# Key and value trees of a hard feed-forward layer: from all leaves for every token to rows sorted by leaf through DRAM

## The chip, the cores and the metric

The kernel runs on one NeuronCore of one Trainium2 chip, as one launch. The metric is the device time of the launch in microseconds. The kernel before was timed three times: 1565.92, 1569.52 and 1570.98 us, median 1569.52 us.

## The reference, cut to what matters

Four transformer layers work on x of 16 x 256 tokens of 128 features (4096 tokens, 32 tiles of 128). The change is in the feed-forward part of the third layer, in which the queries, keys and values of an attention come each out of a tree of depth 4 with 16 leaves. A token goes down a tree by the signs of node scores, and its leaf alone, a small two-layer perceptron of width 64, acts on it:

```python
def _fff(x, node_w, node_b, w1, b1, w2, b2):
    cur = zeros(N)
    for _ in range(4):
        score = einsum('nd,nd->n', xf, node_w[cur]) + node_b[cur]
        cur = 2 * cur + 1 + (score >= 0)
    sel = one_hot(cur - 15, 16)
    hidden = relu(einsum('nd,ldh->lnh', xf, w1) + b1) * sel.T
    return einsum('lnh,lho->no', hidden, w2) + sel @ b2
q, k, v = _fff(x, q_*), _fff(x, k_*), _fff(x, v_*)
attn = softmax(q @ k.T / sqrt(128))        # within each of the 16 batches of 256 tokens
out = attn @ v
```

x is layer-normalised before it enters, and the result is added to x.

## The kernel before, in words

The program is a row of stages, each a block in which every engine has its own instruction stream and engines meet at semaphores; the end of a block holds all of them. In order of time: attention of layer 0, its feed-forward part, a top-k attention (`attention_top`), a routed mixture of 16 experts (`route_top1`, then `run_experts`), attention of layer 2 (`mha`), the trees (`attention_trees`, lines 2017 to 2338), attention of layer 3, and a quantised linear layer.

**The trees before are dense.** `attention_trees` works in 8 groups (g) of 4 tiles, 512 tokens. For each group 24 steps (k) follow, 8 for each of the three trees: a step takes two leaves, 128 hidden columns in all. `hidden` (lines 2074 to 2085) computes them for all 512 tokens by three products of a high and a low part of the weights and the tokens, and a fourth with a one-hot of the tokens' leaves that adds the bias and pushes the hidden values of foreign leaves far below zero, so that the rectifier kills them. ScalarE takes the rectifier (line 2181), VectorE the low part of the result (`low`, line 2284), and `out` (lines 2087 to 2101) multiplies both with the second weights, three products, added up in PSUM over the 8 steps of a tree. TensorE is one step ahead: in step k it issues `hidden` of k+1 before `out` of k. Between the steps of group g lie, written out by hand with step numbers, the attention of group g-1 (`scores`, `turn`, `attend`, one tile after the other) and the routing of group g+1: transposes of x (line 2055), node scores (line 2061), the decisions and one-hots on VectorE (`route`, lines 2243 to 2279). The middle six groups are a hardware loop. GpSimd and the DMA queues have nothing to do in this stage.

**Where the trees' weights come from.** In the routing stage `route_top1` SP loads the weights of all three trees (line 1866) over the space of the experts' weights; ScalarE makes the high parts (line 1729), and VectorE makes the low parts and the bias matrix in 28 pieces (`tree_piece`, lines 1775 to 1798), one in each of the 28 steps of a binary search (`search`, line 1800), between the count (line 1801) and the wait for TensorE's total (line 1803). SP loads the experts' weights behind the last piece (lines 1876 to 1880).

**The same means elsewhere.** `route_top1` sends 32 tiles of rows to places in DRAM by GpSimd's indirect DMAs (line 1887); `mha` of layer 2 gathers 32 tiles of rows with them (line 783). Line 978 loads a register of VectorE from SBUF, ahead of a branch (line 979).

Of the kernel before, what the change touches and what calls it, by code (L numbers as in the profile page):

```python
# [19 lines left out]
P = 128  # L20
# [1022 lines left out]
def attention_top(core):  # L1043
# [5 lines left out]
    with Stage(core, "top") as st:  # L1049
# [12 lines left out]
        names = "xh bo xTp xT qp q S sc top nm P pk PTp PT Y X bn own zero tick".split()  # L1062
        s = {n: st.sem(n) for n in names}
        rs_act, rs_dve = token_scales(core, st, MV[:, :, 1], RS[:], "a")
# [79 lines left out]

        @blk.gpsimd
        def _(pool):
            def slot(b):
# [485 lines left out]
def route_top1(core, masks):  # L1633
# [7 lines left out]
    with Stage(core, "route") as st:  # L1641
# [5 lines left out]
        WC = STEPS * P  # L1647
        raw_w = [core.EW[:, WC * n:WC * n + WC] for n in range(2)]
        raw_mix = [core.EW[:, 2 * WC:2 * WC + MIXC], core.EW[:, 0:MIXC]]
        t1, t2, t3 = (st.sb(n, [P, MIXC], BF16) for n in ("t1", "t2", "t3"))  # L1650
# [9 lines left out]
        names = "xh xTp xT L own cnt tot thr dx ex mvp MTp rowsp dgr eqr ca prf zst sl zfill high piece t1 t2 t3 bw mix0 mix1".split()  # L1660
# [6 lines left out]
        MIXR = (P, SELP)  # L1667
        PIECE, HALF = STEPS * P // 6, MIXC // 2
# [49 lines left out]
        def _(act):  # L1718
# [14 lines left out]
            for n, rows in enumerate(MIXR):  # L1733
                q = slice(0, rows)
                need(act, s["piece"], 12 + 8 * n)
                act.wait_ge(s[f"mix{n}"], 16)
                act.activation(t1[q, :], raw_mix[n][q, :], ACT.Copy).then_inc(s["t1"], 1)
                act.wait_ge(s["piece"], 12 + 8 * n + 2)
                act.activation(t2[q, :], raw_mix[n][q, :], ACT.Copy).then_inc(s["t2"], 1)
                act.wait_ge(s["t1"], n + 1)  # L1740
                act.activation(t3[q, :], t1[q, :], ACT.Identity, scale=core.w("tree", "part")[q, 0:1]).then_inc(s["t3"], 1)
# [3 lines left out]
        def _(dve):  # L1745
            link = Chain(dve, s["own"])
            dve.memset(ones[:], 1.0)
            dve.memset(core.mix[SELP:P, 1, :], 0.0)
# [26 lines left out]
            def tree_piece(k):  # L1775
                need(dve, s["piece"], k)
                if k < 12:
                    n, c = divmod(k, 6)
# [5 lines left out]
                n, step = divmod(k - 12, 8)  # L1784
                step, h = divmod(step, 2)
                q, at = slice(0, MIXR[n]), slice(HALF * h, HALF * h + HALF)
                part = lambda i: core.w("tree", "part")[q, i:i + 1]
# [911 lines left out]
```

## Time and profile before

| what | value |
|---|---|
| median of three runs | 1569.52 us |
| span of the profiled execution | 1580.8 us |
| instructions in the span | 22619 |
| TensorE busy | 1200.3 us (76%) |
| VectorE busy | 999.1 us (63%) |
| ScalarE busy | 612.1 us (39%) |
| GpSimd busy | 275.6 us (17%) |
| moved by DMA | 69.47 MB |

The span goes from the first to the last instruction of one profiled execution, and is the only time shown of that execution; it lies 0.7% above the median of the runs without a profile. Shares of busy time are means over stages that are bound by different engines. An engine's busy time counts an instruction from its start to its modelled end, and instructions of TensorE overlap, so a row's duration of a product is more than what it adds to a stream of products.

### The profile page before, as it was taken

What the parts mean: (1) busy time and instruction counts of PE and PEld (TensorE: products, weight loads), DVE (VectorE), ACT (ScalarE), POOL (GpSimd) and SP (SyncE); (2) the same over time, 40 slices, a digit from 0 to 9 for tenths busy, and PEclk for the clock granted to TensorE, in tenths of its full rate; (3) what the DMA queues carried; (4) which work ended last, traced back from release to release, by engine and by line L of the source; (5) the groups of instructions that cost most, each with busy time, mean ns of one, the idle gap of its engine ahead of it and who ended that gap; (6) DMA issues with size and microseconds to landing.
All of it is one profiled execution on the core that took longest, in us unless ns stands there. A gap on an engine that the chain in (4) does not pass through costs nothing. (4 is left out here: it accounts for less than half of the span.)

```text
span 1580.8 us, 22619 instructions
## 1 busy us (share of the span) xinstructions
PE 1200.3 (76%) x6805; PEld 876.5 (55%) x6805; DVE 999.1 (63%) x3354; ACT 612.1 (39%) x1154; POOL 275.6 (17%) x330
## 2 busy tenths in 40 slices
PE   4788799999766653335826886999999999758852
PEld 2656599899744452114614554677777777335631
DVE  7777746666558859823266775565556665446768
ACT  3465344444332230112225652434444344236631
POOL 1344001010001000071384430000000000024401
PEclk9899799999965555567956996999999999768985
DMA  7342100000000040312224410000000000024301
GB/s 233 105 124 66 28 1 1 2 0 1 1 1 0 0 161 15 108 47 90 71 81 108 111 44 1 1 1 1 1 1 0 0 1 1 1 67 126 98 5 53
DMA packets 54762, 69.47 MB, mean 44 GB/s; under 512 B 6784, under 2 KB 35712, under 8 KB 54016
## 3 DMA queue, kind: packets, MB, share of 16 engines
q1 hardware_dynamic: 51328, 61.78, 13.5%
q0 software_dynamic: 3328, 6.43, 1.3%
q8 instruction: 48, 0.79, 0.2%
q14 instruction: 58, 0.48, 0.1%
HBM read 44.99 MB, written 23.59 MB: 43 GB/s over the span
## 5 line engine op out<-in xcount | busy, mean ns | idle before, releaser
L2284 DVE SCALAR_TENSOR_TENSOR tree_hl<-tree_pH,tree_hh 128x512 fp32r<-128x512 f32 x192 | 132.3, 689 | 94.5 <-ACT tree_hh L2181 92.8
L790 POOL TENSOR_TENSOR mha_ks<-KS,w_ctx 104x1024 fp32r<-104x1024 f32 (+1 forms) x48 | 90.8, 1893 | 535.4 <-POOLq L100 488.6
L2181 ACT ACTIVATE tree_hh<-tree_pH 128x512 fp32r<-128x512 f32 x192 | 114.6, 597 | 145.7 <-PE tree_pH L2085 145.7
L850 DVE TENSOR_REDUCE mha_nm<-mha_pS 128x16 f32<-128x1024 f32 x96 | 117.1, 1220 | 28.3 <-PE mha_pS L612 24.1
L1432 ACT ACTIVATE ffn_hid<-ffn_pH,w_ffn 128x512 f32<-128x512 f32 x128 | 85.5, 688 | 55.1 <-PE ffn_pH L1355 54.4
L2098 PE MATMUL tree_pY<-tree_hh,w2h 128*128 128x512 f32 x192 | 100.9, 526 | 4.3 <-DVE tree_hl L2284 4.2
L733 ACT ACTIVATE XH<-mha_pST 128x1024 f32<-128x1024 f32 x96 | 97.8, 1018 | 9.9 <-PE mha_pST L633 9.8
L612 PE MATMUL mha_pS<-mha_ks,mha_qs 96*128 96x256 f32 (+1 forms) x384 | 79.9, 335 | 27.5 <-DVE mha_nm L850 17.2
L1368 PEld LDWEIGHTS ffn_pE<-W2R,ffn_hid 128*128 128x128 f32 x768 | 94.6, 194 | 4.4 <-issue 0.2
L1544 DVE SCALAR_TENSOR_TENSOR ffn_acc<-ffn_pE,ffn_wt,ffn_acc 128x128 f32<-128x128 f32 x192 | 54.0, 343 | 66.9 <-PE ffn_pE L1368 66.9
L1368 PE MATMUL ffn_pE<-W2R,ffn_hid 128*128 128x128 f32 x768 | 95.2, 278 | 0.0
L612 PEld LDWEIGHTS mha_pS<-mha_ks,mha_qs 96*128 96x128 f32 (+1 forms) x384 | 59.0, 213 | 43.6 <-issue 23.6
L2082 PE MATMUL tree_pH<-tree_xTh,w1h 128*128 128x512 f32 x192 | 80.8, 421 | 1.0 <-DVE tree_sel L2278 1.0
L2084 PE MATMUL tree_pH<-tree_xTh,w1l 128*128 128x512 f32 x192 | 76.6, 399 | 0.0
L2083 PE MATMUL tree_pH<-tree_xTl,w1h 128*128 128x512 f32 x192 | 76.1, 397 | 0.0
L2098 PE MATMUL tree_pY<-tree_hl,w2h 128*128 128x512 f32 x192 | 75.9, 395 | 0.0
L2085 PE MATMUL tree_pH<-tree_sel,mix 128*128 128x512 bf16 x192 | 75.3, 392 | 0.0
L2098 PE MATMUL tree_pY<-tree_hh,w2l 128*128 128x512 f32 x192 | 75.1, 391 | 0.0
L633 PE MATMUL mha_pST<-mha_qs,mha_ks 104*128 104x256 f32 (+1 forms) x384 | 65.5, 295 | 1.5 <-ACT XH L733 0.4
L642 PE MATMUL mha_pO<-XH,VB 128*18 128x256 f32 x768 | 61.3, 392 | 0.0
L1353 PE MATMUL ffn_pH<-ffn_xTh,up_h 128*128 128x512 f32 x128 | 57.7, 451 | 1.6 <-ACT ffn_hid L1432 1.2
L633 PEld LDWEIGHTS mha_pST<-mha_qs,mha_ks 104*128 104x128 f32 (+1 forms) x384 | 55.2, 199 | 3.3 <-ACT XH L733 1.9
(478 smaller groups left out, 2777.4 us busy)
## 6 DMA issues: line engine op xcount, KB each, us to landing
mha_qs<-queries SPq DMA_DIRECT2D x72, 256.0 KB, 4.1
queries<-mha_qh SPq DMA_DIRECT2D x24, 256.0 KB, 2.1
queries<-mha_ql SPq DMA_DIRECT2D x24, 256.0 KB, 2.4
EW<-in_L_W_dram SPq DMA_DIRECT2D x32, 128.0 KB, 2.5
EW<-in_tree_full_dram SPq DMA_DIRECT2D x2, 1536.0 KB, 7.9
slots_in<-route_zero SPq DMA_DIRECT2D x4, 640.0 KB, 11.7
X<-in_x_dram SPq DMA_DIRECT2D x8, 256.0 KB, 7.3
exp_xe<-slots_in SPq DMA_DIRECT2D x16, 128.0 KB, 2.1
```

The lines of the kernel that those rows point to most:

```text
L612: ins = pe.matmul(pS[:, NH * g:NH * g + NH, :], qs[u][0:KC, g, c0:c0 + P], ks[b % KB][0:KC, g, :, :], start=True, stop=True)
L633: ins = pe.matmul(pST[:, n, :], ks[b % KB][0:K1, g, h0:h0 + 2, :], qs[u][0:K1, g, c0:c0 + S], start=True, stop=True)
L733: act.activation(PT[b % PB][:, CU * i:CU * i + CU, :], pST[:], ACT.Exp, scale=SC).then_inc(s["P"], 1)
L790: pool.tensor_tensor(ks[b % KB][0:K1, :, :, :], kb, hb, ALU.mult).then_inc(s["k"], 1)
L850: dve.tensor_reduce(nm[:, t, :], pS[:], AX.X, ALU.max, negate=True).then_inc(s["nm"], 1)
L1368: ins = pe.matmul(pE[p % 2][:, j, :], hc, core.W2R[:, P * r:P * r + P], start=(c == 0), stop=(c == 1))
L1432: act.activation(hid[p % 2][:, c, :], pH[c][:], ACT.Gelu, bias=b).then_inc(s["h"], 1)
L2082: pe.matmul(pH[k % 2][:], core.w1h[:, k0], xTh[u][:], start=True, stop=False)
L2084: pe.matmul(pH[k % 2][:], core.w1l[:, k0], xTh[u][:], start=False, stop=False)
L2098: ins = pe.matmul(bank[:], w2[:, k0], h[k % 2][:], start=(c == 0 and i == 0), stop=False)
L2181: act.activation(hh[k % 2][:], pH[k % 2][:], ACT.Relu).then_inc(s["h"], 1)
L2284: dve.scalar_tensor_tensor(hl[k % 2][:], pH[k % 2][:], 0.0, hh[k % 2][:], ALU.max, ALU.subtract).then_inc(s["lo"], 1)
```

## The change

The query tree stays dense, with 64 steps instead of 192. For the key and the value tree the tokens are sorted by leaf. Each leaf gets whole tiles of 128 rows, so that 48 tiles (32 + 16) hold all tokens of a tree whatever their leaves are. At the start of the stage all 32 tiles are normalised, transposed and scored, and for each token its row in the sorted order is worked out (`running`, `rank`, `starts`, `places`) and for each sorted tile its leaf (`leaf_table`). GpSimd scatters the 32 tiles of rows to DRAM (`core.tx`), once for each tree. In 12 groups of 4 tiles for each tree SP loads the leaf's weights for every tile (a register loaded from the table gives the address) and the 4 tiles of rows; TensorE transposes them (`rows_T`), multiplies up and down (`up`, `down`) in plain fp32, and SP stores the results to DRAM (`core.ty`). GpSimd gathers them back, 32 tiles for each tree, and the attention follows by batches of two tiles. The order is written in slots (`TreeSlots`): 34 slots with a dense step each, 14 for the keys with 7 dense steps, 14 for the values with 11, and then 16 batches of attention with the last 12 dense steps. The sorted rows' space is cleared in the top-k stage, by 12 DMAs of 512 KB. In the routing stage the 28 pieces become 12, and the experts' loads wait for the 12th.

```diff
 def attention_top(core):
+        @blk.sync
+        def _(sp):
+            sp.wait_ge(s["none"], 1)
+            for q in range(2 * NS // (8 * P)):
+                sorted_rows = core.tx[q % 2].rearrange("(q n p) d -> p q n d", n=8, p=P)
+                sp.dma_start(sorted_rows[q // 2], none[:].unsqueeze(1).to_broadcast([P, 8, P])).then_inc(core.rows_cleared, 16)
+            sp.wait_ge(core.rows_cleared, 16 * (2 * NS // (8 * P)))
...
 def route_top1(core, masks):
-            dve.memset(core.mix[SELP:P, 1, :], 0.0)
...
-                tree_piece(k)
+                if k < PIECES:
+                    tree_piece(k)
...
-            sp.wait_ge(s["piece"], BITS)
+            sp.wait_ge(s["piece"], PIECES)
...
+NJ = T + NLEAF
+NS = NJ * P
+XG = NJ // GT
+class TreeSlots:
+    ALONE, SPAN = 34, XG + 2
+    K0, V0 = ALONE, ALONE + SPAN
+    S0 = V0 + SPAN
+    LAG = 3
+    END = S0 + B + LAG + 1
+    def __init__(self):
+        dense = list(range(self.ALONE))
+        dense += [self.K0 + n for n in range(self.SPAN) if n % 2 == 0]
+        dense += [self.V0 + n for n in range(self.SPAN) if n % 4 != 3]
+        dense += [self.S0 + n for n in range(NG * NCH - len(dense))]
...
 def attention_trees(core):
...
+            def rows_T(i):
+                pe.wait_ge(s_rows[i % 3], 16 * (i // 3 + 1))
...
+                for j in range(GT):
+                    ins = pe.transpose(pA[:, cols_of(j)], xs[i % 3][:, j, :], ident)
+                ins.then_inc(s["tr"], 1)
...
+            def up(i):
+                pe.wait_ge(s_leaf[i % 3], 16 * GT * (i // 3 + 1))
+                pe.wait_ge(s["xsT"], i + 1)
+                need(pe, s["hid"], i)
+                for j in range(GT):
+                    ins = pe.matmul(pU[0:LW, cols_of(j)], leaf[i % 3][:, j, 0:LW], xsT[i % 2][:, cols_of(j)], start=True, stop=True)
+                ins.then_inc(s["up"], 1)
...
+            def down(i):
...
+                pe.wait_ge(s["hid"], i + 1)
+                need(pe, s["ys"], i)
+                for j in range(GT):
+                    ins = pe.matmul(pD[:, cols_of(j)], hid[i % 2][:, cols_of(j)], leaf[i % 3][0:LW + 1, j, LW + 1:LEAFC], start=True, stop=True)
+                ins.then_inc(s["dn"], 1)
...
+            for n in range(at.END):
+                m, b = at.step.get(n), at.batch(n)
+                if m is not None and m + 1 < NG * NCH:
+                    hidden(m + 1)
...
+                for lag, part in enumerate((rows_T, up, down)):
+                    i = at.sparse(n, lag)
+                    if i is not None:
+                        part(i)
+                k = at.batch(n, -1)
+                if k is not None and k % 2 == 0:
+                    keys_T(k // 2)
+                if b is not None:
+                    scores(b)
+                if at.batch(n, 1) is not None:
+                    turn(at.batch(n, 1))
+                if m is not None:
+                    out(m)
+                if at.batch(n, at.LAG) is not None:
+                    attend(at.batch(n, at.LAG))
...
+        @blk.gpsimd
+        def _(pool):
...
+            pool.wait_ge(core.rows_cleared, 16 * (2 * NS // (8 * P)))
+            for n in range(2):
+                pool.wait_ge(s["place"], n + 1)
+                for t in range(T):
+                    pool.indirect_dma_start(core.tx[n], bass.IndirectOffsetOnAxis(ap=place[:, n, t:t + 1], axis=0), XH[:, t, :], None,
+                                            bounds_check=NS - 1, oob_is_err=False).then_inc(s_sent[n], 16)
+            for n in range(2):
+                for u in range(2):
+                    pool.wait_ge(s_out[u], 16 * (n + 1) * XG // 2)
+                    if n == 0:
+                        pool.wait_ge(s_sent[u], 16 * T)
+                for t in range(T):
+                    pool.indirect_dma_start((XH, V)[n][:, t, :], None, core.ty[n], bass.IndirectOffsetOnAxis(ap=place[:, n, t:t + 1], axis=0),
+                                            bounds_check=NS - 1, oob_is_err=False).then_inc(s_got[n][t // GT], 16)
+        @blk.sync
+        def _(sp):
+            def load(i):
+                n, j0 = i // XG, GT * (i % XG)
+                if j0 == 0:
+                    sp.wait_ge(s["table"], n + 1)
+                need(sp, s["dn"], i - 2)
+                for j in range(GT):
+                    of = sp.value_load(table[0:1, NJ * n + j0 + j:NJ * n + j0 + j + 1], min_val=0, max_val=NLEAF - 1)
+                    sp.dma_start(leaf[i % 3][:, j, :], core.A["leaves"][n, bass.ds(of, 1), :, :].rearrange("o p c -> p (o c)")).then_inc(s_leaf[i % 3], 16)
+                if j0 == 0:
+                    sp.wait_ge(s_sent[n], 16 * T)
+                sp.dma_start(xs[i % 3][:], core.tx[n][P * j0:P * j0 + GT_P, :].rearrange("(t p) d -> p t d", p=P)).then_inc(s_rows[i % 3], 16)
+            def store(i):
+                n, j0 = i // XG, GT * (i % XG)
+                sp.wait_ge(s["ys"], i + 1)
+                sp.dma_start(core.ty[n][P * j0:P * j0 + GT_P, :].rearrange("(t p) d -> p t d", p=P), ys[i % 2][:]).then_inc(s_out[i % 2], 16)
+            for n in range(2):
+                for i in range(XG * n, XG * n + XG + 2):
+                    if i < XG * n + XG:
+                        load(i)
+                    if i >= XG * n + 2:
+                        store(i - 2)
+        @blk.vector
...
+            def results(i):
+                dve.wait_ge(s["dn"], i + 1)
+                need(dve, s_out[i % 2], 16 * (i // 2))
+                dve.tensor_copy(ys[i % 2][:].rearrange("p t d -> p (t d)"), pD).then_inc(s["ys"], 1)
...
+            for n in range(at.END):
+                m = at.step.get(n)
+                if m is not None:
+                    low(m)
...
+                if n == 1:
+                    starts(1)
+                    places(1)
+                if n in (2, 3):
+                    leaf_table(n - 2)
+                i = at.sparse(n, 0)
+                if i is not None:
+                    rows_T(i)
+                i = at.sparse(n, 2)
+                if i is not None:
+                    results(i)
+                if at.batch(n) is not None:
+                    shift(at.batch(n))
+                done = at.batch(n, at.LAG)
+                if done is not None:
+                    final(done)
+                    statistics(done)
```

## Rows read from the trace of the kernel before

The rows are in the order in which the prediction comes to them. A row of a timeline gives the start in us from the span's start, the duration in us, the engine, the line of the kernel, the operation, what it writes and reads, its shape and its count; a bracket tells how long the engine idled before it and what released it.

**Rows 1.** Windows of the tree stage: busy us (instructions) per engine, granted clock, DMA share, GB/s
```profile
957.30:973.20 15.90, 5.29 (x20) 3.94 (x21) 9.09 (x27) 0.69 (x2) 0.00 (x0) 0.50 0.00 1
973.20:1354.60 381.40, 377.08 (x1759) 268.32 (x1760) 218.55 (x521) 158.65 (x314) 0.00 (x0) 0.99 0.00 1
1354.60:1369.80 15.20, 9.77 (x38) 6.52 (x37) 6.49 (x28) 4.99 (x14) 0.00 (x0) 0.67 0.00 1
```

**Rows 2.** Groups by line, tree stage: busy us, mean ns, idle before and its releaser
```profile
L2284 DVE SCALAR_TENSOR_TENSOR tree_hl<-tree_pH,tree_hh 128x512 fp32r<-128x512 f32 x192 | 132.3, 689 | 94.5 <-ACT tree_hh L2181 92.8
```

**Rows 3.** Timeline of PE: first matmul of two dense steps, four steps apart
```profile
1344.66 0.39 PE L2082 MATMUL tree_pH<-tree_xTh,w1h 128*128 128x512 f32 x1
...
1351.28 0.40 PE L2082 MATMUL tree_pH<-tree_xTh,w1h 128*128 128x512 f32 x1
```

**Rows 4.** Timeline of DVE, routing stage: start us, duration us
```profile
561.50 0.54 DVE L1748 MEMSET mix<- 64x576 uint32 x1 [0.16 <-issue]
...
595.65 0.69 DVE L1782 TENSOR_TENSOR w1l<-EW,w1h 128x512 fp32r<-128x512 f32 x1
596.41 0.22 DVE L1804 TENSOR_SCALAR route_ge<-route_pC,w_route 128x1 f32<-128x1 f32 x1
```

**Rows 5.** Window in the top-k stage: busy us per engine, granted clock, DMA share, GB/s
```profile
535.00:556.00 21.00, 11.75 (x37) 7.25 (x36) 17.85 (x129) 4.39 (x13) 1.45 (x2) 0.50 0.00 0
```

**Rows 6.** Timeline, start of the tree stage, DVE and PE; brackets: idle before
```profile
957.13 0.18 DVE L904 BATCH_NORM_AGGREGATE MV<-mha_bn 128x2 f32<-128x6 f32 x1
...
960.44 1.11 DVE L2238 TENSOR_SCALAR tree_xh<-X,MV,RS 128x128 f32<-128x128 f32 x4 [3.13 <-PEq L100]
...
963.43 1.95 PE L2061 MATMUL tree_pX<-w_tree,tree_xT 128*128 128x48 f32 x8 [0.70 <-ACT tree_xT L2186]
```

**Rows 7.** Timeline of PE, routing stage: the transposes of two successive groups
```profile
575.94 1.09 PE L1682 MATMUL route_pX<-w_ctx,XH 128*128 128x128 f32 x4
...
578.39 1.09 PE L1682 MATMUL route_pX<-w_ctx,XH 128*128 128x128 f32 x4
```

**Rows 8.** Timeline of DVE: operations of 512 and 192 columns out of PSUM
```profile
594.25 0.69 DVE L1772 COPY route_MT<-route_pM 128x512 f32<-128x512 f32 x1 [1.26 <-PE route_pM L1696]
...
965.41 0.36 DVE L2256 TENSOR_TENSOR tree_zs<-tree_pX,w_tree 128x192 f32<-128x192 f32 x1 [0.33 <-PE tree_pX L2061]
```

**Rows 9.** Timeline of POOL: first and last of 32 scatters; the last of 32 gathers
```profile
669.43 1.22 POOL L1887 DMA_INDIRECT slots_in<-XH,slots  x1 [126.06 <-DVE slots L1856]
...
709.25 0.97 POOL L1887 DMA_INDIRECT slots_in<-XH,slots  x1 [0.30 <-issue]
...
838.81 1.00 POOL L783 DMA_INDIRECT XH<-slots_out,slots  x1 [0.31 <-issue]
```

**Rows 10.** Timeline of SP's queue: two of the 32 expert loads
```profile
651.39 0.47 SPq L1878 DMA_DIRECT2D EW<-in_L_W_dram  x1
651.90 0.43 SPq L1879 DMA_DIRECT2D EW<-in_L_W_dram  x1
```

**Rows 11.** The page's DMA issues: count, size, median us from issue to landing
```profile
mha_qs<-queries SPq DMA_DIRECT2D x72, 256.0 KB, 4.1
...
exp_xe<-slots_in SPq DMA_DIRECT2D x16, 128.0 KB, 2.1
...
out_dram<-X SPq DMA_DIRECT2D x8, 256.0 KB, 2.3
```

**Rows 12.** Timeline of DVE around the register load of line 978
```profile
807.20 0.38 DVE L939 BATCH_NORM_AGGREGATE MV<-mha_gbn 128x2 f32<-128x6 f32 x4
808.42 0.37 DVE L954 TENSOR_SCALAR mha_ve<-MV 128x4 f32<-128x4 f32 x1 [0.84 <-issue]
```

**Rows 13.** Timeline of PE after the last dense step: attention products
```profile
1358.98 0.71 PE L2133 MATMUL tree_pO<-tree_vv,tree_PT 128*128 128x128 f32 x4
...
1364.43 1.06 PE L2133 MATMUL tree_pO<-tree_vv,tree_PT 128*128 128x128 f32 x4
```

**Rows 14.** Windows: the expert loads; the attention tail
```profile
655.00:660.00 5.00, 1.22 (x2) 0.21 (x2) 4.52 (x16) 0.00 (x0) 0.00 (x0) 0.50 0.89 264
...
1360.50:1368.40 7.90, 6.45 (x22) 4.49 (x21) 3.91 (x18) 2.28 (x7) 0.00 (x0) 0.50 0.00 0
```

More of the change, by code:

```diff
@@ L1776, in tree_piece @@
                 need(dve, s["piece"], k)
-                if k < 12:
-                    n, c = divmod(k, 6)
+                if k < 4:
+                    n, c = divmod(k, 2)
                     high, low = halves[n]
@@ L2041, in attention_trees @@
+        nm, sm, rc = (st.sb(n, [P, T]) for n in ("nm", "sm", "rc"))
+        bn = two("bn", [P, 6])
         pH = [st.ps(f"pH{u}", [P, 512]) for u in range(2)]
-        pY = [st.ps(f"pY{u}", [P, 512]) for u in range(2)]
-        names = "xh xTp xT xs np own oh ohp sel zero H h lo c Y y vTp v S nm mx P PTp PT O rc X bn mv tick".split()
+        pZ = st.ps("pZ", [P, 4, 512])
+        pS, pT = st.ps("pS", [P, 512]), st.ps("pT", [P, 512])
+        pY, pA, pU, pD = (pZ[:, n, :] for n in range(4))
+        names = "const early full ones xh xTp xT np go own hot ran cnt rank place table xs ohp sel H h lo c Y y tr xsT up hid dn ys ktp kt S nm P PTp PT O rc X bn".split()
@@ L2213, in group @@
-            def group(g, u):
-                for k in range(STEPS):
-                    hidden(g, u, k)
-                    if k == 0 and past(g):
-                        out(g - 1, 1 - u, 2)
-                    if k in (NCH, 2 * NCH):
-                        out(g, u, k // NCH - 1)
-                    if past(g):
-                        attention(g - 1, 1 - u, k)
-                    if k == 14 and more(g):
-                        x_evac(g + 1, 1 - u)
-            rs_act(act)
-            x_evac(0, 0)
@@ L2331, in _, with normalise @@
-            normalise(0, 0)
-            dve.memset(oh[:], 0.0).then_inc(s["zero"], 1)
-            rs_dve(dve)
-            for step in range(7):
-                route(0, 0, step)
-            group_slots(dve, group)
-            for k in range(STEPS):
-                attention(NG - 1, 1, k)
-MAGIC = 1.5 * 2.0 ** 23
+            link = Chain(dve, s["own"])
+            def normalise(g):
+                for t in range(GT * g, GT * g + GT):
+                    ins = dve.tensor_scalar(XH[:, t, :], X[:, t, :], MV[:, t, 0:1], RS[:, t:t + 1], ALU.subtract, ALU.mult)
+                ins.then_inc(s["xh"], 1)
@@ new lines, in statistics @@
+            def statistics(b):
+                dve.wait_ge(s["X"], b + 1)
+                for t in range(TB * b, TB * b + TB):
+                    ins = dve.bn_stats(bn[t % 2][:], X[:, t, :])
+                ins.then_inc(s["bn"], 1)
+                dve.wait_ge(s["bn"], b + 1)
+                for t in range(TB * b, TB * b + TB):
+                    dve.bn_aggr(MV[:, t, :], bn[t % 2][:])
+            for u in range(2):
+                ins = dve.memset(hid[u][LW:LW + 1, :], 1.0)
+            ins.then_inc(s["ones"], 1)
@@ new lines, in _ @@
+            ins.then_inc(s["hot"], 1)
+            link(path(2, 2))
+            running(1)
+            starts(0)
+            places(0)
+            for n in range(at.END):
+                m = at.step.get(n)
+                if m is not None:
+                    low(m)
+                    g, c = divmod(m, NCH)
+                    if c == 3 and 1 <= g < NG - 1:
+                        split(g + 1)
+                if n == 1:
[7 more added lines that the diff above has]
+                i = at.sparse(n, 2)
+                if i is not None:
+                    results(i)
+                if at.batch(n) is not None:
+                    shift(at.batch(n))
[3 more added lines that the diff above has]
+                    statistics(done)
```

602 lines of the change are left out of this document (327 added, 275 removed).

## The prediction

> **What bounds the kernel now.** I read first the engines and the time slices of the page: TensorE is 76% busy, but its share moves from stage to stage, so no mean over the span prices this change. The page's chain that ended last covers a few per cent only, inside the last stage, and says nothing of the trees. Then I took windows around the tree stage, the only large one that the diff rebuilds [rows 1]: from 957.3 to 1369.8 us, 412.5 us, of which 381.4 are dense steps with TensorE 377.1 us busy at full clock and no transfer at all. The groups by line show who waits there: ScalarE and VectorE idle for TensorE, and VectorE's `low`, 0.689 us a step, for ScalarE [rows 2]; the reader is to see that TensorE is the bound. The timeline gives the price of a dense step: 6.62 us for four, so 1.655 us [rows 3].
>
> **The change, part by part.**
>
> Gone: 128 of 192 dense steps, 128 x 1.655 = 212 us of a full engine. This is the whole gain; the rest is what is put in its place.
>
> *Routing stage.* The 16 pieces that go run beside TensorE's total: a piece lies from 595.65 to 596.34 and the next operation starts at 596.41 anyway [rows 4]. I cost them at nothing; the cover, TensorE's answer, stays. One memset of 0.54 us goes from ahead of the statistics [rows 4]: -0.5. The experts' loads start 16 steps earlier beside idle queues: nothing.
>
> *Clearing.* 6.3 MB in the top-k stage are 24 us at the 264 GB/s of the experts' loads [rows 14]; the stage is on VectorE (17.9 of 21 us busy) with no DMA [rows 5], and SP has nothing else there: nothing. Without that cover it would be 24 us.
>
> *Head.* Before, the first dense step began 15.9 us after the last stage [rows 1]. Now all 8 groups come first. 3.3 us to the first normalisation and 1.1 for it [rows 6], about 1 for two new memsets. Then transposes and node products of 8 groups, like the routing stage's, which go at 2.45 us a group [rows 7], plus 0.2 because the node products take 1.95 us [rows 6] and I give the narrower ones there 1.75: 8 x 2.65 = 21.2. Then VectorE alone: 512 columns cost 0.69 us, 192 cost 0.36 [rows 8], so about 1 ns a column. Two operations of 1536 columns (3.5), six on the paths (2.2), three one-hots, three copies and two scans of 512 (5.5), the starts (1.2), three of 512 for the places (2.3): 14.7, of which I take 14, as some are bf16. Sum 41 us.
>
> *34 dense slots.* 34 x 1.655 = 56.3; slots 1 to 3 carry `places` and the two leaf tables, some 3 us each on VectorE ahead of `low`, less what a slot has room for (+5.5); selections and a start at half clock (+2): 64 us. The scatter of the keys, 31 intervals in 39.8 us [rows 9], so 41 for 32 rows of tiles, ends inside it, and that of the values lies beside the key slots.
>
> *24 sorted groups, where it is decided.* The queue's program is load(i), store(i-2), load(i+1). The store waits for `results`(i-2), VectorE's copy behind `down`(i-2), and TensorE issues that in the slot whose first instruction is `rows_T`(i). So load(i+1) can't be issued before load(i) has landed and a whole slot has gone by: three buffers, and yet nothing is ahead. The interval of two groups is the sum of this circle:
> - TensorE: four transposes 1.09 us [rows 7], and `up` and `down`, 8 products of two passes each. Four passes take 0.71 us at full clock and 1.06 at half [rows 13]; half gives 4 x 1.06 = 4.2. Which clock? After the last dense step products with gaps let it fall to half in the window's 7.9 us, though TensorE is busy for 6.45 of them [rows 14]. Here it waits longer: half. 5.3.
> - VectorE's copy of 512 columns 0.7 [rows 8]; the store's issue 0.45 [rows 10].
> - four times a register load and an issue. An issue is 0.43 to 0.47 [rows 10]. A register load of SP is not in the trace. From above: 0.84 us of VectorE hold a load, a comparison and a semaphore [rows 12]; from below: 0.30, the gap between two of GpSimd's transfers [rows 9]. They are near each other, so the middle, 0.57. 4 x 1.02 = 4.1.
> - the rows' landing: 2.3 us for 256 KB, between 2.1 for 128 KB and 4.1 among other transfers [rows 11]; three hand-overs 0.3.
>
> Sum 13.2 us. The Trainium skill's page "DMA: Bandwidth & Descriptors" (Latency and other measured facts) gives such a load a floor of about 600 ns. By it the circle would be 13.3 us, and its cheap end would fall away; no row here shows the load by itself.
>
> DMA itself is not the bound: 0.9 MB a group are 3.4 us at 264 GB/s [rows 14]. Nine intervals of each tree go round, as three loads are ahead at its start: 18 x 13.2 = 238 us. Beside them: the keys' first three slots 9 and last two 7; for the values, whose first load stands behind the keys' last store on the queue, 7.3 until rows land, two more loads 9.1, a slot 6, the last two 7. Sum 45. The 18 dense steps in these slots cost nothing, hidden by the wait for the rows.
>
> *Attention.* The values' gather waits for the last store: 0.45 and 2.3, four gathers at 1.3 [rows 9] and 1.7 to land, 9.6 us; the other 28 gathers (2.6 us a batch) hide behind the engines. Nine batches with a dense step: 1.655 and about 2.5, as VectorE's `final` stands ahead of the next `low`: 38. Four without, at half clock, 16. The last three slots and statistics 7.5. Sum 71. The keys' gather (42 us) lies beside the value slots.
>
> Total: 41 + 64 + 238 + 45 + 71 = 459 us against 412.5, less 0.5: **46 us more**. The terms are of one execution with a span of 1580.8 us, the one time shown of it, 0.7% above the median of 1569.5; I put the difference on the median: **1615 us**.
>
> **The rivals.**
>
> *A short circle (not slower).* The place is the same circle. Outside of it the stage takes 221 us, so at 10.7 us an interval 18 of them make no difference, and below that the kernel is faster. Full clock (0.55 + 2.8 for TensorE) and register loads of 0.30 give 10.1 us; with the other sparse slots 6 us shorter, 215 + 182 = 397, so 1554 us. For it: both prices are ends of rows. Against: the clock falls under less waiting than here [rows 14].
>
> *The queue runs ahead.* If loads came as fast as SP issues them, a group would cost 4 x 1.02 + 0.9 = 5 us: 41 + 64 + 120 + 10 + 71 = 306, so 1463 us. Against it stands the order of the program; only if I misread that order can it be.
>
> *A dear circle.* Register loads of 0.84 and landings of 4.1 us [rows 11, 12] give 16.1 us, 52 more: 1667 us. For it: a bounds check and a computed address come with each load, and 64 scatters and gathers run beside. Against: the queues are nearly empty.
>
> That the change would do less than it says is excluded: 24 groups run whatever the leaves are.
>
> **How the numbers follow.** Differences below 0.3% (5 us) can't be told from no change. The forecast 0.60, short 0.14, ahead 0.06, dear 0.20. Slower: all of dear, 0.56 of the forecast; faster: ahead, 0.11 of short, 0.02 of the forecast; the rest no change. The forecast's own range is 1575 to 1650 (the clock may rise in some slots, the head and the attention may be off by 15). Down to the short circle's 1552 and up to 1667 some 2 in 10 are left out: ahead, half of dear and a little of short.
>
> **What would show it.** In the profile after: no leaf load issued in a tree's later groups before the store of two groups earlier; intervals of 12 to 14.5 us between two such stores; TensorE waiting for the rows at `rows_T`, at a clock near 0.5; register loads as gaps of about half a microsecond on SP; 40 us before the first dense step; 71 after the last store. Stores 5 us apart, or a clock near 1 in those slots, would prove the forecast wrong; so would a dense stretch that waits for the scatter.

## The result, and the profile after

The changed kernel takes 1635.6 us (median of 4 runs, 1632.6 to 1638.4) against 1568.6 us of the kernel before in runs beside it: a ratio of 1.043, 95% interval 1.041 to 1.045. It is 67 us slower; forecast were 46 more, 1615 us in a range of 1552 to 1667. Medians leave out one slow run, of 4456.3 us, of the variant with the store behind the next load.

The tree stage of the changed kernel in four windows (busy us and instructions per engine, granted clock, DMA share, GB/s), cut where the stage before ends, at VectorE's first `low`, at the first transposes of sorted rows, at the last `down` and at the last statistics:

```profile
945.40:988.30 42.90, 26.42 (x117) 22.94 (x118) 23.84 (x70) 6.72 (x12) 2.21 (x8) 0.51 0.00 1
988.30:1062.00 73.70, 70.81 (x268) 41.98 (x267) 35.68 (x60) 26.16 (x44) 55.80 (x57) 1.00 0.25 77
1062.00:1350.50 288.50, 153.44 (x604) 113.01 (x604) 46.10 (x70) 36.34 (x115) 40.06 (x40) 0.59 0.29 78
1350.50:1419.20 68.70, 63.38 (x374) 49.57 (x371) 41.04 (x141) 36.92 (x103) 32.00 (x32) 1.00 0.13 36
sum 473.80, PE 314.05 PEld 227.50 DVE 146.66 ACT 106.14 POOL 130.08; mean PE 78.51 PEld 56.88 DVE 36.66 ACT 26.54 POOL 32.52
```

These answer to the three windows of [rows 1]. The stage takes 473.8 us where it took 412.5. TensorE has less to do (314 us busy against 392), but in the third window, that of the 24 sorted groups, it is busy for 153 of 288.5 us, and its granted clock is 0.59. So the dense work that was to go is gone, and the groups more than took its place.

Who waits there stands in the page's groups (busy us, mean ns, idle before and its releaser) and in its list of DMA issues (KB each, median us to landing):

```profile
L2167 PE MATMUL tree_pZ<-w_ctx,tree_xs 128*128 128x128 f32 x96 | 24.9, 409 | 134.9 <-DMA tree_xs<-leaf_rows 134.7
...
tree_leaf<-in_leaves_dram SPq DMA_DIRECT2D x96, 96.5 KB, 2.0
...
tree_xs<-leaf_rows SPq DMA_DIRECT2D x24, 256.0 KB, 3.0
leaf_results<-tree_ys SPq DMA_DIRECT2D x24, 256.0 KB, 2.3
```

TensorE idles for 134.9 us ahead of the transposes of sorted rows, nearly all of it for the rows' DMA (134.7), which lands 3.0 us after its issue. More than half of such a wait lies ahead of the issue: of the 6.87 us at 1119.57 below, 3.8 pass before the rows are issued at 1116.51 us and 3.1 after. SP's queue and TensorE's timeline over one round (start us, duration, engine, line, what, count; brackets: idle before):

```profile
1097.43 0.38 SPq L2378 DMA_DIRECT2D leaf_results<-tree_ys  x1
1098.58 4.02 SPq L2370 DMA_DIRECT2D tree_leaf<-in_leaves_dram  x4
1102.64 0.67 SPq L2373 DMA_DIRECT2D tree_xs<-leaf_rows  x1
1111.64 0.38 SPq L2378 DMA_DIRECT2D leaf_results<-tree_ys  x1
1112.78 3.69 SPq L2370 DMA_DIRECT2D tree_leaf<-in_leaves_dram  x4
1116.51 0.43 SPq L2373 DMA_DIRECT2D tree_xs<-leaf_rows  x1
```

```profile
1105.86 1.11 PE L2167 MATMUL tree_pZ<-w_ctx,tree_xs 128*128 128x128 f32 x4 [7.91 <-DMA tree_xs<-leaf_rows]
1106.91 1.97 PE L2175 MATMUL tree_pZ<-tree_xsT,tree_leaf 128*64 128x128 f32 x8
1108.81 2.08 PE L2184 MATMUL tree_pZ<-tree_leaf,tree_hid 65*128 65x128 f32 x8
...
1119.57 1.12 PE L2167 MATMUL tree_pZ<-w_ctx,tree_xs 128*128 128x128 f32 x4 [6.87 <-DMA tree_xs<-leaf_rows]
```

Follow it round: rows of a group here at 1105.86; transposes, `up` and `down` of TensorE to 1110.89 (5.03 us); VectorE's copy and the hand-overs to the store at 1111.64 (0.75); the store 0.38; from its end to the rows' issue, with four register loads and four leaf issues between, 4.49; from the rows' issue to the next transposes 3.06. Sum 13.71 us. Stores of the keys' groups 0 and 8 are issued at 1070.04 and 1179.73 us, so the mean of eight intervals is 13.71 us too. The forecast had 13.2. All nine intervals of each tree are 13.7 and 13.6 us on the mean, so 13.7 is taken below.

### The profile page after: what moved, and what is told of

It is laid out like the page before. It is cut to its first block and busy times, and to the rows that moved or that the text cites. A ratio compares the mean times of both kernels' runs of the same rounds, so it can differ in the third digit from the quotient of the medians.

```text
span 1630.4 us, 21584 instructions
## 1 busy us (share of the span) xinstructions
PE 1119.4 (69%) x6345; PEld 824.8 (51%) x6347; DVE 901.1 (55%) x3102; ACT 547.1 (34%) x1095; POOL 408.6 (25%) x467
## 5 line engine op out<-in xcount | busy, mean ns | idle before, releaser
L2167 PE MATMUL tree_pZ<-w_ctx,tree_xs 128*128 128x128 f32 x96 | 24.9, 409 | 134.9 <-DMA tree_xs<-leaf_rows 134.7
L2462 DVE COPY tree_xsT<-tree_pZ 128x512 f32<-128x512 f32 x24 | 16.6, 691 | 172.6 <-PE tree_pZ L2167 172.6
L2284 ACT ACTIVATE tree_hid<-tree_pZ,tree_leaf 64x128 f32<-64x128 f32 x96 | 27.0, 356 | 248.0 <-PE tree_pZ L2175 248.0
L733 ACT ACTIVATE XH<-mha_pST 128x1024 f32<-128x1024 f32 x96 | 97.8, 1019 | 10.9 <-PE mha_pST L633 10.8
L2167 PEld LDWEIGHTS tree_pZ<-w_ctx,tree_xs 128*128 128x128 f32 x96 | 16.0, 204 | 145.9 <-DMA tree_xs<-leaf_rows 144.9
L612 PEld LDWEIGHTS mha_pS<-mha_ks,mha_qs 96*128 96x128 f32 (+1 forms) x384 | 59.6, 215 | 42.6 <-issue 19.8
L2350 POOL DMA_INDIRECT leaf_rows<-XH,tree_place x64 | 63.3, 989 | 57.4 <-DVE tree_place L2442 38.2
L2457 DVE SCALAR_TENSOR_TENSOR tree_hl<-tree_pH,tree_hh 128x512 fp32r<-128x512 f32 x64 | 43.8, 685 | 48.3 <-ACT tree_hh L2274 48.1
L2358 POOL DMA_INDIRECT XH<-leaf_results,tree_place x32 | 32.6, 1018 | 141.0 <-DMA leaf_results<-tree_ys 131.5
L1892 POOL DMA_INDIRECT slots_in<-XH,slots x32 | 32.6, 1020 | 135.1 <-DVE slots L1863 125.6
L1471 POOL TENSOR_TENSOR X<-X,ffn_xh 128x512 f32<-128x512 f32 (+1 forms) x8 | 10.3, 1285 | 208.9 <-DVE ffn_xh L1501 208.9
L2358 POOL DMA_INDIRECT tree_V<-leaf_results,tree_place x32 | 32.0, 1000 | 118.6 <-DMA leaf_results<-tree_ys 109.1
```

Of the source, the lines that this page charges most:

```text
L612: ins = pe.matmul(pS[:, NH * g:NH * g + NH, :], qs[u][0:KC, g, c0:c0 + P], ks[b % KB][0:KC, g, :, :], start=True, stop=True)
L733: act.activation(PT[b % PB][:, CU * i:CU * i + CU, :], pST[:], ACT.Exp, scale=SC).then_inc(s["P"], 1)
L2350: pool.indirect_dma_start(core.tx[n], bass.IndirectOffsetOnAxis(ap=place[:, n, t:t + 1], axis=0), XH[:, t, :], None, bounds_check=NS - 1, ...
L2358: pool.indirect_dma_start((XH, V)[n][:, t, :], None, core.ty[n], bass.IndirectOffsetOnAxis(ap=place[:, n, t:t + 1], axis=0), bounds_check= ...
```

## Experiments

Times are medians. Each variant is the changed kernel with the edit shown, and all of them are alike up to the trees. The last four are built on one another: the spread steps on the variant that runs ahead, the two queues on "Both together".

**The kernel before, once more.**

> The kernel before once more, unchanged. The profiled execution that the prediction read is 14 us longer than the timed runs, and it enters the tree stage at 957.3 us, where the changed kernel and four variants of it enter it at 943 to 946. Theory 1: those 12 us are that one execution's own, in the experts and the second attention ahead of the trees; then this execution enters the trees near 945 us, the tree stage still takes 412 us, and the span is about 1568 us. Theory 2: the changed kernel gains them, by the experts' loads that start earlier; then this one enters near 957 us again, with a span near 1580 us.

It took 1572.0 us in this one run (1569.1 is the median of nine others beside it), with a span of 1570.2. VectorE's last L904 of the stage ahead starts at 946.7 us, and the tree stage is:

```profile
946.90:1359.60 412.70, 392.43 (x1816) 278.89 (x1816) 234.20 (x575) 164.34 (x330) 0.00 (x0) 0.96 0.00 1
```

Theory 1: the 12 us ahead of the trees belong to the execution that the prediction read. The tree stage is 412.7 us here as there, so its change is 473.8 - 412.7 = 61.1 us, and spans differ by 60.2. The 67 us between the medians are 6 more; the profiled run of the changed kernel is the shortest of its four, and this one of the kernel before lies 3 us above its median, so I take these 6 us for spread; no run shows where they lie.

**The store behind the next load.**

```diff
-                for i in range(XG * n, XG * n + XG + 2):
+                for i in range(XG * n, XG * n + XG + 3):
                     if i < XG * n + XG:
                         load(i)
-                    if i >= XG * n + 2:
-                        store(i - 2)
+                    if i >= XG * n + 3:
+                        store(i - 3)
```

> SP's order becomes load(i+1), store(i-2); all else stays. Theory A, the prediction's (the store's place in the queue is what holds the next load back): with the store out of the way the loads run ahead, and groups follow each other by SP's own time, about 6 us apart instead of 13.6 (4 register loads and issues 3.7 us, the rows' issue 0.4, the store 1.2). Some 20 intervals get 7.6 us shorter: 1636 - 150 = about 1485 us. Theory B (the circle is closed by the three leaf buffers as well: load(i+1) also waits for down(i-2), which stands in the same TensorE slot behind the transposes of group i): only VectorE's copy 0.7 and the store's issue 0.4 leave the circle, so intervals of 12.5 us, and 1636 - 20 x 1.1 = about 1614 us.

1614.0 us (three runs), ratio 1.027 (1.023 to 1.030). SP's queue:

```profile
1107.66 3.68 SPq L2370 DMA_DIRECT2D tree_leaf<-in_leaves_dram  x4
1111.38 0.43 SPq L2373 DMA_DIRECT2D tree_xs<-leaf_rows  x1
1111.86 0.51 SPq L2378 DMA_DIRECT2D leaf_results<-tree_ys  x1
1119.70 3.68 SPq L2370 DMA_DIRECT2D tree_leaf<-in_leaves_dram  x4
```

Theory B. The store no longer stands ahead of the load, and yet the next leaf load comes no earlier than TensorE's `down` allows: a `down` ends at 1106.92 us, and the load that needs its buffer is issued at 1107.66, a register load later. Leaf loads begin at 1068.95 and, five groups later, at 1132.42 us: intervals of 12.7 us. The store's place is worth some 20 us, not the whole wait: the same circle is closed a second time by the leaf buffers, as `load(i+1)` needs the buffer that `down(i-2)` reads.

**Leaves fixed, no register loads.** The result uses wrong leaves' weights, of the same size.

```diff
-                    of = sp.value_load(table[0:1, NJ * n + j0 + j:NJ * n + j0 + j + 1], min_val=0, max_val=NLEAF - 1)
-                    sp.dma_start(leaf[i % 3][:, j, :], core.A["leaves"][n, bass.ds(of, 1), :, :].rearrange("o p c -> p (o c)")).then_inc(s_leaf[i % 3], 16)
+                    of = (j0 + j) % NLEAF
+                    sp.dma_start(leaf[i % 3][:, j, :], core.A["leaves"][n, of:of + 1, :, :].rearrange("o p c -> p (o c)")).then_inc(s_leaf[i % 3], 16)
```

> The leaf of each tile is a constant of the program, so SP loads no register; the weights are those of wrong leaves, the same number of bytes in the same transfers. In the trace of the changed kernel the four leaf issues of a group start 1.1 us apart, 0.44 of which is the issue, and the first starts 0.77 us after the store's end. If the register loads are in the circle, as the prediction has it at 0.57 each, an interval loses 4 x 0.66 to 0.76 = 2.6 to 3.0 us: 10.8 us, and some 20 intervals give about 55 us: 1580 us. If they are hidden beside other work (rival: the interval is set by landings or by TensorE), no change, 1636 us.

1578.0 us, ratio 1.005 (1.003 to 1.006).

```profile
1101.66 0.38 SPq L2378 DMA_DIRECT2D leaf_results<-tree_ys  x1
1102.08 1.98 SPq L2370 DMA_DIRECT2D tree_leaf<-in_leaves_dram  x4
1104.10 0.44 SPq L2373 DMA_DIRECT2D tree_xs<-leaf_rows  x1
1111.82 0.38 SPq L2378 DMA_DIRECT2D leaf_results<-tree_ys  x1
```

The register loads are in the circle. From the store's end to the rows' issue it is 2.06 us, where it was 4.49: 2.43 for four, 0.61 us each. The edit takes away the loads and the run-time addresses together, but the addresses cost nothing that can be seen: in the variant that runs ahead, below, four issues with run-time addresses and their loads set apart take 1.93 us, here 1.98. The nine intervals of each tree are 10.7 and 10.9 us on the mean, so 10.8 where it was 13.7. That is 0.4 more than the 2.43, as the clock rose in part of the shorter waits: five intervals from 1080.81 to 1132.44 us are 10.3 us, and `down` takes 1.3 to 1.4 us in them instead of 2.08 (the granted clock is 0.63 in the window of 1100 to 1180 us, against 0.50 there in the changed kernel).

**TensorE busy while it waits.** 28 products that nothing uses fill the wait.

```diff
                     i = at.sparse(n, lag)
+                    if lag == 0 and i is not None and i % XG > 2:
+                        for _ in range(28):
+                            pe.matmul(pS[:], identb[:], upto[:, 0, :, :].rearrange("p l t -> p (l t)"), start=True, stop=True)
```

> 28 products of 128 by 512 bf16 into a bank that is free in these slots stand ahead of the transposes of every group but the first three of each tree, where TensorE waits 7 to 8 us now. They compute nothing that is used. Theory: the circle holds 5.1 us of TensorE at half clock; kept busy, the clock rises to full, the transposes, up and down take 2.8 us, and an interval 11.3 us: 18 x 2.3 = 41 us less, 1595 us. The fill takes about 6 us at full clock and fits the wait. Rival 1: the clock stays at half; then the fill takes 12 us and each interval grows to about 18 us, 1710 us. Rival 2: the clock rises but the intervals stay at 13.6 us, because they are set by SP and the transfers alone: 1636 us.

1594.9 us, ratio 1.016 (1.014 to 1.019).

```profile
1111.38 0.66 PE L2167 MATMUL tree_pZ<-w_ctx,tree_xs 128*128 128x128 f32 x4 [1.39 <-DMA tree_xs<-leaf_rows]
1111.97 1.09 PE L2175 MATMUL tree_pZ<-tree_xsT,tree_leaf 128*64 128x128 f32 x8
1112.98 1.16 PE L2184 MATMUL tree_pZ<-tree_leaf,tree_hid 65*128 65x128 f32 x8
```

The window of 1100 to 1180 us (busy us and instructions per engine, granted clock, DMA share, GB/s):

```profile
1100.00:1180.00 80.00, 66.67 (x355) 38.65 (x359) 13.85 (x21) 12.44 (x39) 0.00 (x0) 0.99 0.29 81
```

The granted clock is 0.99, TensorE's share of the circle falls from 5.03 to 2.76 us, and stores are issued at 1103.58, 1114.90 and 1126.18 us: 11.3 us apart. Over the nine intervals of each tree the mean is 11.6 and 11.8 us, as one of the first nine and two of the second take 12.5 to 13.8. So the half clock is a price inside the circle, and 41 us in all, bought back with work that does nothing.

**The rows issued ahead of the leaves.**

```diff
                 need(sp, s["dn"], i - 2)
+                if j0 == 0:
+                    sp.wait_ge(s_sent[n], 16 * T)
+                sp.dma_start(xs[i % 3][:], core.tx[n][P * j0:P * j0 + GT_P, :].rearrange("(t p) d -> p t d", p=P)).then_inc(s_rows[i % 3], 16)
                 for j in range(GT):
...
-                if j0 == 0:
-                    sp.wait_ge(s_sent[n], 16 * T)
-                sp.dma_start(xs[i % 3][:], core.tx[n][P * j0:P * j0 + GT_P, :].rearrange("(t p) d -> p t d", p=P)).then_inc(s_rows[i % 3], 16)
```

> Inside a load the rows' transfer is issued ahead of the four leaf loads. Theory B: TensorE needs the rows of a group at the start of a slot, its leaves only a slot later, so the four register loads and issues (from the end of the store to the rows' issue, 4.5 us) leave the circle: intervals of 13.6 - 4.4 = 9.2 us, about 20 of them, 1636 - 88 = about 1548 us, below the kernel before. Rival: the rows only move, and the leaf landing (2.0 us behind an issue that now ends later) becomes the late one at up(i): then intervals stay above 12 us and the time above 1600 us.

1546.8 us, ratio 0.984 (0.981 to 0.987): 1.6% below the kernel before, by moving one transfer in the queue.

```profile
1106.42 0.38 SPq L2378 DMA_DIRECT2D leaf_results<-tree_ys  x1
1106.85 0.51 SPq L2370 DMA_DIRECT2D tree_xs<-leaf_rows  x1
1108.44 3.68 SPq L2373 DMA_DIRECT2D tree_leaf<-in_leaves_dram  x4
1115.68 0.38 SPq L2378 DMA_DIRECT2D leaf_results<-tree_ys  x1
```

(The lines' numbers have moved: L2370 is the rows' issue here.) The rows are issued 0.4 us after the store's issue instead of 4.9; seven intervals from 1070.51 to 1133.74 are 9.0 us each. What is needed first had been issued last.

**The selector product on 128 rows.** This one is for the dense phase, which took 73.7 us and not 64.

```diff
-    core.mix = sb("mix", [SELP, MIXC], BF16)
+    core.mix = sb("mix", [P, MIXC], BF16)
...
-        selq = st.sb("selq", [SELP, T * P], BF16)
+        selq = st.sb("selq", [P, T * P], BF16)
...
+            pool.memset(core.mix[SELP:P, :], 0.0).then_inc(s["early"], 1)
+            pool.wait_ge(s["early"], 1)
+            pool.memset(selq[SELP:P, :], 0.0).then_inc(s["early"], 1)
+            pool.wait_ge(s["early"], 2)
```

> The changed kernel with its selector product on 128 rows instead of 64, the upper 64 filled with zeros on both sides (two memsets by GpSimd ahead of the statistics). In the trace of the changed kernel a dense step takes 1.905 us where the prediction took 1.655 from the kernel before: the weight load of the 64-row product starts 0.36 us after the load before it ended, and the next one 0.23 us after that, where loads otherwise lie beside the matmul before. Theory: the change of row count costs this; then a step is 1.655 us again, 34 slots give 8.5 us and the attention's steps up to 3: 1624 to 1628 us. Rival: the gap belongs to the bf16 type or the semaphore on that product and stays: 1636 us.

1621.6 us, ratio 1.035 (1.032 to 1.037), a little below the 1624 to 1628 expected. TensorE's matmuls (PE) and weight loads (PEld) around the product, first of the changed kernel, then of this variant; a bracket is the idle time before:

```profile
1045.11 0.40 PE L2144 MATMUL tree_pH<-tree_xTh,w1h 128*128 128x512 f32 x1
...
1045.58 0.39 PE L2146 MATMUL tree_pH<-tree_xTh,w1l 128*128 128x512 f32 x1
1045.89 0.09 PEld L2147 LDWEIGHTS tree_pH<-tree_selq,mix 64*128 64x128 bf16 x1 [0.36 <-issue]
1045.90 0.39 PE L2147 MATMUL tree_pH<-tree_selq,mix 64*128 64x512 bf16 x1
1046.21 0.19 PEld L2156 LDWEIGHTS tree_pZ<-tree_hh,w2h 128*128 128x128 f32 x1 [0.23 <-issue]
...
1047.01 0.40 PE L2144 MATMUL tree_pH<-tree_xTh,w1h 128*128 128x512 f32 x1
```

```profile
1034.23 0.40 PE L2144 MATMUL tree_pH<-tree_xTh,w1h 128*128 128x512 f32 x1
...
1034.69 0.40 PE L2146 MATMUL tree_pH<-tree_xTh,w1l 128*128 128x512 f32 x1
1034.92 0.10 PEld L2147 LDWEIGHTS tree_pH<-tree_selq,mix 128*128 128x128 bf16 x1 [0.27 <-issue]
1034.92 0.39 PE L2147 MATMUL tree_pH<-tree_selq,mix 128*128 128x512 bf16 x1
1035.07 0.19 PEld L2156 LDWEIGHTS tree_pZ<-tree_hh,w2h 128*128 128x128 f32 x1
...
1035.86 0.40 PE L2144 MATMUL tree_pH<-tree_xTh,w1h 128*128 128x512 f32 x1
```

From L2146's start to the next product's weights it is 0.63 us with 64 rows and 0.38 with 128: 0.25 us a step. Dense steps (L2144) begin 1.90 us apart in the changed kernel and 1.63 here; on the mean of six steps, from 1034.23 to 1044.15 us, it is 1.65, as in [rows 3]. From the end of the stage ahead to the first transposes of sorted rows it is 109 us instead of 117, and the stage is 8 us shorter; the other 6 us of the difference between the medians lie outside it (this kernel's profiled run enters the trees 4 us earlier), so I don't count them. The price is that of the row count: the type bf16 and the semaphore on the product are the same in both.

**SP's program anew, running ahead.**

```diff
-            for n in range(2):
-                for i in range(XG * n, XG * n + XG + 2):
...
+            for i in range(3):
+                leaf_load(i)
+            for i in range(2):
+                rows_load(i)
+            for k in range(2 * XG + 2):
+                if 3 <= k + 1 < 2 * XG:
+                    leaf_load(k + 1)
+                if k >= 2:
+                    store(k - 2)
+                if k + 2 < 2 * XG:
+                    rows_load(k + 2)
```

`leaf_load` loads its four registers, then waits for `down` of three groups earlier and issues; `rows_load` waits for the transposes of three groups earlier only. Buffers and slots are as they were.

> SP's program is written anew, buffers and slots are those of the changed kernel: a group's rows are issued as soon as the transposes of three groups earlier are done, so two slots before they are needed; its four register loads stand ahead of the wait for the leaf buffer; the leaves are needed a slot after the rows. Theory: the circle is then open, and a slot costs what SP or TensorE need, the larger: SP 4 x (0.67 + 0.44) + 0.4 + 0.4 = 5.3 us, TensorE 2.8 us at full clock or 5.3 at half, plus a dense step in 18 of 28 slots. Slots of 5.5 to 7 us in place of 13.6: 24 of them, and 4 short ones, in 150 to 175 us in place of 289, so 1496 to 1522 us. Rival: what stays behind one another is the transfers' landing (3.0 for rows, 2.0 for leaves) and not the order; then slots stay above 9 us, as with the rows issued first, and the time near 1547 us.

1482.3 us, ratio 0.946 (0.944 to 0.948): 14 us below the expected range, as the sparse slots take 137 us (1064.0 to 1201.2) and not 150 to 175.

```profile
1089.84 1.93 SPq L2373 DMA_DIRECT2D tree_leaf<-in_leaves_dram  x4
1091.81 0.43 SPq L2385 DMA_DIRECT2D leaf_results<-tree_ys  x1
1092.29 0.51 SPq L2380 DMA_DIRECT2D tree_xs<-leaf_rows  x1
1095.52 1.93 SPq L2373 DMA_DIRECT2D tree_leaf<-in_leaves_dram  x4
```

This group takes 5.7 us; from 1073.27 to 1188.44 us nineteen of them are 6.1 on the mean, as seven of them take 6.2 to 7.1. SP hardly rests: from the end of the rows' issue to the next leaf issue it is 2.72 us, four register loads of 0.68. Three buffers were enough; the order was not.

**The dense steps spread.**

```diff
-    ALONE, SPAN = 34, XG + 2
+    ALONE, SPAN = 24, XG + 2
...
-        dense += [self.K0 + n for n in range(self.SPAN) if n % 2 == 0]
-        dense += [self.V0 + n for n in range(self.SPAN) if n % 4 != 3]
+        dense += [self.K0 + n for n in range(self.SPAN)]
+        dense += [self.V0 + n for n in range(self.SPAN)]
```

> As the variant that runs ahead, and the dense steps are spread: 24 alone, then one in each of the 28 sparse slots (before 34, and 18 in the 28). Theory: the slots are SP's (5.3 us), TensorE at full clock has room for a dense step of 1.9 in each, and ten slots of about 2 us less stand ahead: 18 to 22 us below the variant that runs ahead, about 1480 to 1500 us. The rows of the first group, whose scatter ends 43 us into the dense phase, come as the 24 slots end (24 x 1.9 = 46 us). Rival: TensorE is the bound of the slots, so the steps cost there what they cost alone: no difference.

1463.1 us, ratio 0.933 (0.931 to 0.934): 19 us below the variant that runs ahead, within the 18 to 22 expected, so the sparse slots take ten more dense steps for nothing. From the first to the last transposes it is 128.3 us with them (1045.4 to 1173.7) and 128.9 without (1064.0 to 1192.9).

**Both together.** The 128-row product, and 26 steps alone (`ALONE = 26`), 10 beside the attention.

> The variant with the dense steps spread, with the selector product on 128 rows, 26 steps alone and 10 beside the attention (24 and 12 there). Theory: the 26 steps of 1.655 us take 2.5 us less than 24 of 1.905, two steps fewer lie beside the attention at 1.655 or more each, and the ten left there save up to 0.25 each: 5 to 9 us below 1463, so 1454 to 1458 us. In the sparse slots nothing changes, as SP paces them at 6.0 us a group. Rival: the first rows, whose scatter ends near 1031 us, become the late ones, and what the steps save is waited for: 1460 us or more.

1452.6 us, ratio 0.925 (0.923 to 0.928), 10.5 below the variant with the dense steps spread, a little more than expected. First and last transposes lie 129.3 us apart (1041.0 to 1170.3): SP paces them still, as the next variant shows.

**Half of the leaves on ScalarE's queue.**

```diff
+            def leaf_load(i):
...
+                of = [act.value_load(table[0:1, NJ * n + j0 + j:NJ * n + j0 + j + 1], min_val=0, max_val=NLEAF - 1) for j in (2, 3)]
+                need(act, s["dn"], i - 2)
+                for j in (2, 3):
+                    act.dma_start(leaf[i % 3][:, j, :], core.A["leaves"][n, bass.ds(of[j - 2], 1), :, :].rearrange("o p c -> p (o c)")).then_inc(s_leaf[i % 3], 16)
```

> The combined variant, with two of a group's four leaf loads (register loads and issues) on ScalarE's queue, behind its leaf activations. Theory: in the variants that run ahead SP never rests in a sparse slot (four register loads 2.5 to 3.2, leaf issues 1.9, store and rows 1.0: 6.0 us); with half of the leaves gone it needs 3.5, ScalarE 4.2, TensorE at full clock 4.4 to 4.8 us: slots of 4.6 us, 24 x 1.3 = 31 us less, about 1425 us. Rival: the slots are set by transfers, 0.9 MB a group: then they stay near 6 us, and the time within 5 us of the combined variant.

1435.1 us, ratio 0.914 (0.911 to 0.917): 17.5 us below, where some 30 were expected. From the first to the last transposes it is 101.9 us where it was 129.3, and TensorE is the bound (window as above):

```profile
1060.00:1140.00 80.00, 76.17 (x480) 59.61 (x486) 37.62 (x59) 31.92 (x91) 33.19 (x35) 1.00 0.82 228
```

The DMA engines come next, at a share of 0.82. But the first transposes start at 1050.3 us, 9.3 later than in the variant with both:

```profile
1017.43 0.60 ACT L2274 ACTIVATE tree_hh<-tree_pH 128x512 fp32r<-128x512 f32 x1 [1.04 <-PE tree_pH L2147]
1018.89 5.05 ACTq L2295 DMA_DIRECT2D tree_leaf<-in_leaves_dram  x6
1024.34 1.08 ACT L2274 ACTIVATE tree_hh<-tree_pH 128x512 fp32r<-128x512 f32 x2 [6.31 <-issue]
```

The six leaf loads of the first three groups keep ScalarE from its `hh` (the rectifier of a dense step) for 6.3 us, and the dense steps wait.

**The first three groups' leaves on SP again.**

```diff
-                if n == 12:
-                    for i in range(3):
-                        leaf_load(i)
...
-                return [sp.value_load(table[0:1, NJ * n + j0 + j:NJ * n + j0 + j + 1], min_val=0, max_val=NLEAF - 1) for j in range(2)]
+                return [sp.value_load(table[0:1, NJ * n + j0 + j:NJ * n + j0 + j + 1], min_val=0, max_val=NLEAF - 1) for j in range(GT if i < 3 else 2)]
```

> The variant with two queues, but all leaves of the first three groups are issued by SP again, before the scatter has ended. In its trace the six leaf loads of these groups keep ScalarE from 1018.0 to 1024.3 us, and the first sorted group starts at 1050.3 us where the combined variant starts it at 1041.0; from there the sparse slots last 101.9 us against 129.3. Theory: that stall is the 9 us by which it started late; without it the first group starts near 1041 to 1044 us, and the time is 1435 - 7 to 9 = 1426 to 1428 us. Rival: the late start has another cause (the rows' transfers, SP), and the time stays at 1435 us.

1428.1 us (1425.4 to 1432.3), ratio 0.910 (0.909 to 0.912). From the end of the stage ahead to the first transposes it is 96.6 us where it was 103.5, and the rest is as it was. This is the best of the versions: 9% below the kernel before, and 208 us below the changed one.

## Why the prediction was right, and where it was off

- **The cause.** Right: nothing runs ahead, TensorE waits at `rows_T` for rows that are issued a whole round after the last, at a clock near a half. The signs named in advance are all there: intervals of 13.7 us (12 to 14.5), clock 0.59 over all sparse slots and 0.50 within the later groups of the keys, 42.9 us before the first dense `low` (40), 67.9 us after the last store's issue at 1351.3 us (71), and the first rows, issued at 1031.8 us, were not waited for.
- **Who holds the next load back.** Half right. The prediction gave the store the whole of it. With the store out of the way the interval fell only by 1.0 us; the leaf buffers hold the load back just the same, since a load asked for rows and leaves together while the rows' buffer was free a slot and more earlier. That, and not the store, is what the order had to part.
- **The terms of the circle.** TensorE 5.0 (5.3 forecast), copy and hand-overs 0.75 (1.0), store 0.38 (0.45), register loads and leaf issues 4.5 (4.1), landing 3.1 (2.3, the lower of the two rows of 256 KB in [rows 11]). Each register load costs 0.61 us by the run without them, where 0.57 was taken. The Trainium skill's page "DMA: Bandwidth & Descriptors" (Latency and other measured facts) gives such a load (`tensor_load` there) a floor of about 600 ns; the 0.61 agrees with it. That the forecast's 0.57 came so near is luck in part: it was the middle of 0.30 and 0.84, which lie almost a factor of three apart and are of other engines. So is part of the sum: TensorE, copy and store were 0.6 us too dear, loads and landing 1.2 too cheap. The nine intervals of each tree took 123.3 and 122.6 us, so 7.9 more than the 238; the remaining sparse slots 42.6 instead of 45.
- **The dense slots: the step that failed.** 34 slots at 1.655 us from [rows 3], with 7.5 for the rest, made 64; it was 73.7. The price of the step was carried over from a product of 128 rows to one of 64, and a step became 1.905 us: 34 x 0.25 = 8.5 of the 9.7 us. Fewer rows looked like less work.
- **The sum.** Of the 14.8 us by which the stage is longer than the forecast 459, the dense slots are 9.7, the circle 7.9, the head 1.9, less 2.4 for the other sparse slots and 2.3 for the attention (68.7 from the last `down`, 71 forecast).
- **What was put at nothing.** The stages ahead ended when they did before (945.3 us against 946.9), which is inside the spread of 7 us of the executions below, so clearing, routing pieces and experts' loads cost and gave nothing that can be seen.
- **The rivals.** The short circle needed full clock and cheap register loads at once; each was run by itself, 1594.9 and 1578.0 us. The first leaves 11.7 us an interval on the mean. The second, with no register load at all, leaves 10.8, about the break-even of 10.7, and came out 0.5% slower: the rest of the stage, dense slots above all, took 225 us there where the break-even had 221. Of the dear circle neither price came: 0.61 us and not 0.84 for a register load, 3.1 and not 4.1 for the landing. The queue that runs ahead was shut out by this program's order, as said; in another order it is what happens, at 6.1 us a group where 5 was worked out.

## What to carry to other kernels

In a pipeline with buffers, go round one whole circle: from a transfer's issue through its consumers to the event that lets the next be issued. The interval is the sum of that circle, here in spite of three buffers, until some load is issued on an event that lies an iteration or more back; give each transfer the wait of its own buffer, and issue first what is needed first. And a cut of work pays only as far as the queue that issues what replaces it keeps up: here 128 dense steps less cost 67 us, and gave 142 once SP's program was in order, the slots filled, the product padded and half of the leaves issued by ScalarE.

## What the hardware showed that was not expected

- A product of 64 rows between products of 128 costs 0.25 us more than the same product padded to 128 rows with zeros. The Trainium skill's page "TensorE: Matmul & The Clock Gate" (LDWEIGHTS (loading the stationary operand)) says that a weight load's time goes by its columns and not by its rows; the loads' own durations agree, 0.09 against 0.10 us. What differs is when they start: both the load of the 64-row weights and that of the weights behind them began later. No run here tells why.
- A register load from a table in SBUF holds SP's queue for 0.61 to 0.68 us, more than the issue that it serves, of which four without such loads take 1.98 us.
- The changed kernel and its variants, alike up to the trees, entered them between 940.8 and 948.2 us. The kernel before entered them at 946.7 us in one execution and at 957.1 in the one that the prediction read. So a stage's time is compared within the stage.
